# Turns of q and k in score banks, bias parts through DRAM, logits and router steps over groups, w2 casts moved forward

## The chip, the cores and the metric

One core of one Trainium2 chip. The metric is the device time of one execution in microseconds (us). The engines are PE (TensorE, matmuls and transposes), DVE (VectorE), ACT (ScalarE), POOL (GpSimd) and SP (SyncE, which issues the DMAs here).

## What is computed

Four blocks in a row on x of 4 batches x 256 tokens x 512, each added to x. `_layernorm` has no weights.

```python
x = x + attention(_layernorm(x))     # 32 heads of 16, causal, alibi; out @ w_proj + b_proj
x = x + ffn(_layernorm(x))           # 3 experts, top 2
x = x + mlp(_layernorm(x))           # gate/up/down over 1376, smallest half of |silu| set to 0
x = x + ffn(_layernorm(x))           # the same experts and weights again

# attention
scores = einsum('bqhd,bkhd->bhqk', q, k) / 16 + slopes * (k_pos - q_pos)   # causal
out = softmax(scores) @ v
# ffn
modality_ratio = mean(abs(h[:, 76:])) / (mean(abs(h[:, :76])) + 1e-08)     # of each batch
gate_logits = concat([h, modality_ratio]) @ gate_w + gate_b
top_val, top_idx = top_k(softmax(gate_logits), 2)     # weights of each token, normalised
pre = einsum('bsd,edf->ebsf', h, w1) + b1
act = [tanh(pre[0]), gelu(pre[1]), silu(pre[2])]
expert_out = einsum('ebsf,efd->ebsd', act, w2) + b2
# the two experts are those that the batch's first token chooses
```

## The kernel before, in words

All engines run orders written out by hand, and `need(engine, signal, step, k)` makes an engine wait until a signal has been given often enough. What is queued behind a waiting instruction on its engine waits too. 128 tokens are a row (T=8 rows, TB=2 to a batch), 4 heads a group (NG=8 groups to a batch). PSUM has eight banks. Banks 0 to 2 and 3 to 5 are the two score slots (`slot`), banks 6 and 7 are `work`.

**Products in parts.** A projection multiplies float32 in two parts, high (a cast) and low (the difference): `project` (L1566) makes 12 matmuls, `rowsT_hi` by `wqkv_hi`, `rowsT_hi` by `wqkv_lo`, `rowsT_lo` by `wqkv_hi`. ACT makes high parts (`turned_rows` L719, `attention_high` L731, `weight_high` L787), DVE low parts (`turned_rows_low` L979, `attention_low` L991, `weight_low` L1294).

**q and k.** The scores take q and k in three bf16 parts. For each batch PE turns them in four steps (`turn` L1602: f=0 q and f=1 k of the first 16 heads, f=2 and 3 of the last 16). Even steps use `work[0]`, odd ones `work[1]`. ACT casts a turned bank to the first part (L745), DVE subtracts it (`residues` L1007), ACT casts the residue to the second part (`second_part` L752), POOL subtracts that for the third (`cut` L635). `turn(b, 2)` and `turn(b, 3)` wait for the residue that frees their bank, and so does what next uses the bank: `value(0, j)` in batch 0, `project_heads(b-1, j)` afterwards. SP writes the parts to DRAM (`write_cuts` L513) and gathers them back head by head into `qst` and `kst` (`gather` L522), 12 DMAs for each half of the heads.

**A batch.** PE makes the causal scores of each group (`scores` L1635), DVE two row maxima of each (`maxima` L1018). Between groups the value projection, the turn of the heads of the batch before and its low parts, the row turns and q and k of the next batch have their places (`steady` L1155). The maxima are cut, turned in bank 0 and sent by SP into `qst`. Then PE makes transposed scores (`scores_t` L1662), ACT exponentials (L763), PE products with v (`weigh` L1684, two banks in turn) and turns them back (`back` L1699), DVE copies and normalises (`attend` L1040). Ahead of this stand the rest of the next batch's turns and both output projections of the batch before (`project_heads` L1623), whose sums DVE adds to x (`x_plus` L1073). Into the groups of `attend` DVE also takes layer norms, for batch 1 on, and:

- `gate_means` (L1105, batch 0, group 1): two operations over 1536 columns that take the mean off the gate weights.
- `logit_rows` (L1084, groups 4 and 6 of batches 1 to 3): three sums for each row of tokens. A batch's rows are taken in the attention of the next batch. Row 6 and row 7 are taken in the first two expert rows (`ffn_dve` L1361).
- the router of batches 0 and 1 (L1213, L1238, L1260), in groups 2, 3 and 5 of batch 3.

**Biases.** b_proj and b1 enter the products as a matmul with three bf16 parts on partitions 0, 32 and 64 of `bias_proj` and `bias1`. DVE clears `b_raw` (L1133), SP loads both biases into three partitions of it, and `cut_bias` (L1092) makes the parts with six operations, once for 512 and once for 1536 columns, between `query(1, 0)` and the maxima of batch 0.

**Experts.** `ffn_front` (L1731) makes both chosen experts' pre-activations of a row (two blocks of 12 matmuls and a bias), ACT the functions, DVE the mix, PE turns it and `ffn_back` (L1761) multiplies by w2. The first row's front stands ahead of the output projections of batch 3, the w2 casts (L790) and subtractions (L1297) in the first round of `ffn_act` and `ffn_dve`.

## Time and profile before

| | |
|---|---|
| median of 3 runs | 751.97 us (751.32 to 753.47) |
| profiled execution | 751.89 us, its span 750.1 us |
| mean granted PE clock | 0.972 |
| PE busy | 677.2 us (90%) |
| DVE busy | 497.1 us (66%) |
| ACT busy | 333.1 us (44%) |
| POOL busy | 82.6 us (11%) |
| DMA | 51.84 MB, mean 69 GB/s |

The span runs from the first to the last instruction of the profiled execution; its own time is 1.8 us longer. Busy shares are means over stages with different limits, so the stages are read one by one: the attention batches up to about 275 us, the first experts to about 400, the MLP, and the second experts. "Idle before" in a row is how long the engine had nothing to do, with what ended it. The granted clock is a share of full speed.

### The profile page before, as it was taken

What the parts mean: (1) busy time and instruction counts of PE and PEld (TensorE: products, weight loads), DVE (VectorE), ACT (ScalarE), POOL (GpSimd) and SP (SyncE); (2) the same over time, 40 slices, a digit from 0 to 9 for tenths busy, and PEclk for the clock granted to TensorE, in tenths of its full rate; (3) what the DMA queues carried; (4) which work ended last, traced back from release to release, by engine and by line L of the source; (5) the groups of instructions that cost most, each with busy time, mean ns of one, the idle gap of its engine ahead of it and who ended that gap; (6) DMA issues with size and microseconds to landing.
All of it is one profiled execution on the core that took longest, in us unless ns stands there. A gap on an engine that the chain in (4) does not pass through costs nothing.

```text
span 750.1 us, 9861 instructions
## 1 busy us (share of the span) xinstructions
PE 677.2 (90%) x3656; PEld 485.3 (65%) x3656; DVE 497.1 (66%) x916; ACT 333.1 (44%) x510; POOL 82.6 (11%) x185
## 2 busy tenths in 40 slices
PE   5768799889889878899999989999999989999996
PEld 3546467657657656687777746656657546687875
DVE  4678577388468866878678364564562795878655
ACT  4200530441353446252355995674671923525221
POOL 4200200210210101101015000100100210000000
PEclk9899999999999999899999999999999999999999
DMA  8273530350552504000044000000000404000000
GB/s 282 79 215 116 157 99 1 88 170 1 145 188 92 213 1 151 1 0 1 1 151 151 0 1 0 1 0 1 1 1 6 163 0 168 1 15 29 15 29 28
DMA packets 31058, 51.84 MB, mean 69 GB/s; under 512 B 2729, under 2 KB 16425, under 8 KB 29455
## 3 DMA queue, kind: packets, MB, share of 16 engines
q1 hardware_dynamic: 31010, 51.21, 20.7%
q8 instruction: 30, 0.49, 0.3%
q14 instruction: 18, 0.15, 0.1%
HBM read 42.61 MB, written 8.39 MB: 68 GB/s over the span
## 4 chain that ended last, share of the span: by engine, by line
PE 71%; DVE 20%; issue 3%; ACT 3%; DMA 2%; POOL 1%; SPq 0%; ACTq 0%; DVEq 0%; POOLq 0%
PE ps L1781 12%; PE ps L1920 11%; PE ps L1748 11%; PE ps L1981 8%; PE ps L1575 6%; PE ps L1924 5%; DVE nmax L1025 3%; PE ps L1627 2%; DVE junk L1087 2%; PE ps L1689 2%; DMA wqkv_raw<-in_L_attn_a_w_attn 2%; PE ps L1757 2%; DVE nmax L1022 1%; DVE prodT L1510 1%; PE ps L1650 1%
## 5 line engine op out<-in xcount | busy, mean ns | idle before, releaser
L1981 PE MATMUL ps<-wdT,prodT 128*128 128x512 f32 (+1 forms) x176 | 80.1, 612 | 0.3
L763 ACT ACTIVATE probsT<-ps 128x1536 f32<-128x1536 f32 x32 | 45.9, 1450 | 37.8 <-PE ps L1679 37.6
L1981 PEld LDWEIGHTS ps<-wdT,prodT 128*128 128x128 f32 (+1 forms) x176 | 33.8, 196 | 41.9 <-issue 39.7
L802 ACT ACTIVATE funs<-ps 128x512 f32<-128x512 f32 x16 | 9.6, 598 | 97.4 <-PE ps L1750 83.4
L1087 DVE SCALAR_TENSOR_TENSOR junk<-x_sb,gate_row 128x512 f32<-128x512 f32 x48 | 41.5, 865 | 1.6 <-DVE failed L1429 0.3
L1510 DVE COPY prodT<-ps 128x512 f32<-128x512 f32 (+1 forms) x24 | 13.8, 599 | 43.0 <-PE ps L1970 42.7
L647 POOL TENSOR_SCALAR ln_spread<-ln_moments 128x1 f32<-128x1 f32 x24 | 6.0, 250 | 317.5 <-DVE ln_moments L1082 317.4
L1355 DVE SCALAR_TENSOR_TENSOR x_sb<-b_row,coef,x_sb 128x512 f32<-128x512 f32 x48 | 37.9, 790 | 1.7
L1025 DVE TENSOR_REDUCE nmax<-ps 128x4 f32<-128x1024 f32 x32 | 38.8, 1212 | 0.0
L745 ACT CAST parts<-ps 128x512 bf16<-128x512 f32 x16 | 9.4, 587 | 65.1 <-PE ps L1612 64.9
L912 ACT ACTIVATE sign_junk<-mlp_size_next,minus_guess 128x1376 bf16<-128x1376 f32 x24 | 34.6, 1443 | 0.8
L912 ACT ACTIVATE sign_junk<-mlp_size_main,minus_guess 128x1376 bf16<-128x1376 f32 x24 | 34.6, 1442 | 0.8
L1575 PE MATMUL ps<-wqkv_hi,rowsT_hi 128*128 128x512 f32 x96 | 30.4, 442 | 3.5 <-DVE oT_lo L988 1.6
L845 ACT CAST aT_hi<-ps 128x512 fp32r<-128x512 f32 x32 | 17.2, 591 | 34.2 <-PE ps L1757 34.2
L640 POOL TENSOR_TENSOR parts<-resid,parts 128x512 bf16<-128x512 f32 x16 | 18.2, 1162 | 125.4 <-ACT parts L755 125.4
L1689 PE MATMUL ps<-probsT,v_ones 128*32 128x256 f32 x256 | 21.1, 401 | 11.7 <-DVE o_tok L1048 8.4
L1054 DVE COPY outT<-ps 128x256 f32<-128x256 f32 x32 | 13.6, 424 | 26.1 <-PE ps L1694 25.8
L1291 DVE TENSOR_TENSOR aT_lo<-ps,aT_hi 128x512 fp32r<-128x512 f32 x32 | 20.6, 684 | 12.7 <-ACT aT_hi L845 12.6
L1575 PE MATMUL ps<-wqkv_lo,rowsT_hi 128*128 128x512 f32 x96 | 27.3, 407 | 1.1 <-DVE wqkv_lo L993 1.1
L1575 PE MATMUL ps<-wqkv_hi,rowsT_lo 128*128 128x512 f32 x96 | 26.3, 395 | 0.0
L1352 DVE TENSOR_TENSOR x_sb<-ps,x_sb 128x512 f32<-128x512 f32 x16 | 11.1, 691 | 22.6 <-PE ps L1781 22.5
L1679 PE MATMUL ps<-qst,kst 107*128 107x256 bf16 x128 | 25.1, 277 | 0.0
(282 smaller groups left out, 1709.3 us busy)
## 6 DMA issues: line engine op xcount, KB each, us to landing
cuts<-parts SPq DMA_DIRECT2D x16, 384.0 KB, 3.1
qst<-cuts SPq DMA_DIRECT2D x48, 128.0 KB, 2.6
kst<-cuts SPq DMA_DIRECT2D x48, 128.0 KB, 2.6
w_first_raw<-in_L_ffn_w SPq DMA_DIRECT2D x6, 1024.0 KB, 7.8
w_second_raw<-in_L_ffn_w SPq DMA_DIRECT2D x6, 1024.0 KB, 8.5
wqkv_raw<-in_L_attn_a_w_attn SPq DMA_DIRECT2D x3, 1024.0 KB, 9.6
wdT<-in_L_attn_b_w_down SPq DMA_DIRECT2D x1, 2560.0 KB, 10.3
wg_raw<-in_L_attn_b_w_gate SPq DMA_DIRECT2D x1, 2048.0 KB, 8.0
```

The source lines that it names most:

```text
L763: nc.scalar.activation(probsT[:, g % 2, :].rearrange("p (k n) -> p k n", k=3), slot[g % 2], ACT.Exp).then_inc(exp_ok.sem, 1)
L912: nc.scalar.activation(sign_junk[:, :], size_rows(n)[1][:, :], ACT.Sign, bias=minus_guess[:, i:i + 1], accum_out=probe_sum[:, i:i + 1]).th ...
L1025: nc.vector.tensor_reduce(nmax[:, 1, g * G:(g + 1) * G], sl[:, 1:3, :].rearrange("p s (h k) -> p (s h) k", h=2), AX.X, ALU.max, negate=Tru ...
L1087: nc.vector.scalar_tensor_tensor(out=junk[:, :], in0=x_sb[:, t, :], scalar=1.0, in1=gate_v[:, 0:D, e], op0=ALU.mult, op1=ALU.mult, accum_o ...
L1355: nc.vector.scalar_tensor_tensor(out=x, in0=b2_row[:, e, :], scalar=coef[:, n, e:e + 1], in1=x, op0=ALU.mult, op1=ALU.add).then_inc(ffn.b2 ...
L1575: last = nc.tensor.matmul(bank, rows[:, c, at_j], weight[:, n, c, :], start=(i == 0 and c == 0), stop=(i == 2 and c == KC - 1))
L1689: nc.tensor.matmul(o_ps[32 * i:32 * i + 2 * HD, 0:S], v_ones[:, 0, h, :], probsT[:, g % 2, D + i * S:D + (i + 1) * S], start=True, stop=Fa ...
L1748: nc.tensor.matmul(ps[:, 2 * i + s, :], a[:, i, c, :], part[:, e, c, :], start=(k == 0 and c == 0), stop=False)
L1781: last = nc.tensor.matmul(ps[:, Y_BANK, :], a[:, s, c, :], part[:, e[s], c, :], start=(k == 0 and c == 0), stop=(k == len(products) - 1 an ...
L1920: last = nc.tensor.matmul(ps[:, first_bank + q, :], a[:, c, :], part[:, c, at_q], start=(k == 0 and c == 0), stop=(k == 2 and c == KC - 1))
L1924: last = nc.tensor.matmul(ps[:, first_bank + q, 0:IT], row_whole[:, c, :], end[:, c, :], start=(c == 0), stop=(c == KC - 1))
L1981: last = nc.tensor.matmul(ps[:, Y_BANK, :], prodT[0:m, c, :], wdT[0:m, c, :], start=(c == 0), stop=(c == IC - 1))
```

## The change

- The turns of a batch go to four banks of the score slots (2 to 5 in batch 0, 0, 1, 3 and 4 later), the turned maxima to bank 2. A turn waits for no residue; the first two transposed scores of the attention before wait for them. `turn(1, 0)` moves behind `key(1, 1)`. On DVE of batch 0, `query(0, 1)` and `key(0, 1)` come earlier and the residues directly after them.
- In batches 1 and 2 PE makes the first output projection after the second turn, and the second one inside the attention, after the first transposed scores. DVE's x sums stand between the residues.
- The key gathers of batch 0, 12 of 24, are issued by ACT, six ahead of the row casts of batch 1 and six behind them.
- The biases are loaded as 16 columns on 128 partitions, cut there by four DVE operations ahead of `attention_low(1)`, written to DRAM and loaded back as rows.
- `gate_means` is done by ACT in batch 1, in seven operations.
- The logit sums stand one to a group (two more after the last group of batch 1, four behind the last head turns); the last part of the router's weights is a step of its own, one group later.
- At the experts, the first row's front is cut in two around the output projections of batch 3, and ACT's w2 casts and DVE's subtractions come earlier.

```diff
-        maxima_bank = ps[:, 0, :].bitcast(BF16)
+        maxima_bank = ps[:, 2, :].bitcast(BF16)
+        def turn_bank(b, f):
+            return ps[:, (2, 3, 4, 5)[f] if b == 0 else (0, 1, 3, 4)[f], :]
+        def send_rows(eng, b, half, side):
+            stack = (qst, kst)[side]
+            hs = slice(half * H // 2, (half + 1) * H // 2)
+            for t, term in enumerate(TERMS):
+                eng.dma_start(stack[t:TROWS:len(TERMS), hs, :],
+                              cuts[side, half, term[side]].rearrange("(d h) t -> d h t", d=HD)
+                              ).then_inc(scat[half].sem, 16)
...
@@ SP
             load_part(1)
+            sp.dma_start(bias_cols[0:D // NBIAS, :], b_proj.rearrange("(p n) -> p n", n=NBIAS)).then_inc(bias_in, 16)
+            sp.dma_start(bias_cols[D // NBIAS:P, :], b1_in.rearrange("e (p n) -> (e p) n", n=NBIAS)
+                         ).then_inc(bias_in, 16)
             sp.dma_start(x_sb[:, TB:2 * TB, :], x_v[:, TB:2 * TB, :]).then_inc(x_next, 16)
...
-            sp.wait_ge(bias_zero, 1)
+            sp.wait_ge(bias_cut, 4)
+            sp.dma_start(bias_cuts.rearrange("i (p n) -> p i n", p=P), bias_parts[:, :, :]).then_inc(bias_out, 16)
+            sp.wait_ge(bias_out, 16)
+            sp.wait_ge(bias_zero, 2)
             for i in range(3):
-                row = b_raw[32 * i:32 * i + 1]
...
+                sp.dma_start(bias_proj[32 * i:32 * i + 1, :], bias_cuts[i:i + 1, 0:D]).then_inc(bias_rows, 16)
+                sp.dma_start(bias1[32 * i:32 * i + 1, :, :].rearrange("a e n -> a (e n)"),
+                             bias_cuts[i:i + 1, D:]).then_inc(bias_rows, 16)
...
-            gather(0, 0)
-            gather(0, 1)
+            gather(0, 0, (0,))
+            gather(0, 1, (0,))
@@ ACT
-            cut(0, range(4))
+            first_part(0, 0)
+            first_part(0, 1)
+            second_part(0, 0)
+            first_part(0, 2)
+            second_part(0, 1)
+            first_part(0, 3)
+            second_part(0, 2)
+            second_part(0, 3)
+            need(act, cuts_out[0], 0, 16 * 2)
+            send_rows(act, 0, 0, 1)
             turned_rows(1)
+            need(act, cuts_out[1], 0, 16 * 2)
+            send_rows(act, 0, 1, 1)
...
-                cut(b + 1, (0,))
+                if b == 1:
+                    gate_means()
+                first_part(b + 1, 0)
                 maxima(b)
-                cut(b + 1, (1, 2, 3))
+                first_part(b + 1, 1)
+                for f in range(2):
+                    second_part(b + 1, f)
+                for f in range(2, 4):
+                    first_part(b + 1, f)
+                for f in range(2, 4):
+                    second_part(b + 1, f)
                 attend(b)
...
+            need(act, y_ps, B - 1, TB)
+            second_weights(w2_first, 0, (0, 1))
+            ffn_act(ffn1, norm2, route1, lambda: second_weights(w2_first, 0, (2,)), to_mlp)
@@ DVE, attend: what stands in a group
-                    elif b >= 1 and g in (4, 6):
-                        logit_rows(route1, (b - 1) * TB + (g - 4) // 2)
-                    if b == 0 and g == 1:
-                        gate_means()
+                    if b == B - 1:
+                        if g == 2:
+                            router.scores()
+                        elif g == 3:
+                            router.ranks()
+                        elif g in (4, 7):
+                            logit_row(route1, (b - 1) * TB, (g - 4) // 3)
+                        elif g == 5:
+                            router.weights()
+                        elif g == 6:
+                            router.middle_weights()
+                    elif b == 1:
+                        if g in (2, 4, 6, 7):
...
+                    elif b >= 2 and g >= 2:
+                        logit_row(route1, (b - 1) * TB + (g - 2) // E, (g - 2) % E)
...
                 normalise(NG - 1)
+                if b == 1:
+                    for e in (1, 2):
+                        logit_row(route1, (b - 1) * TB + 1, e)
@@ DVE
             for j in range(TB):
                 turned_rows_low(0, j)
+            cut_biases()
             attention_low(1)
...
             key(0, 0)
+            query(0, 1)
             dve.wait_ge(x_next, 16)
             ln_moments_of(1)
-            query(0, 1)
+            key(0, 1)
+            for f in range(4):
+                residue(0, f)
             ln_rows(1)
-            nc.vector.memset(b_raw[0:65, :], 0.0).then_inc(bias_zero, 1)
-            key(0, 1)
-            residues(0)
...
-            cut_bias(0, D, bias_proj[0:65, :], 0)
-            cut_bias(D, NBIAS, bias1[0:65, :, :].rearrange("p e n -> p (e n)"), 6)
...
+                residue(b + 1, 0)
+                residue(b + 1, 1)
                 if b >= 1:
-                    for j in range(TB):
-                        x_plus(b - 1, j)
+                    x_plus(b - 1, 0)
+                residue(b + 1, 2)
+                residue(b + 1, 3)
+                if b >= 1:
+                    x_plus(b - 1, 1)
                 attend(b)
...
                 turned_heads_low(B - 1, j)
+            for e in range(2, 2 + E + 1):
+                logit_row(route1, (B - 2) * TB + e // E, e % E)
...
                 norm_stats(norm2, (B - 1) * TB + j)
+                weight_low(w2_first, w2_high, w2_low, 0, j)
             mix(ffn1, route1, 0, 0)
-            ffn_dve(ffn1, route1, norm3, lambda: second_weights(w2_first, 0), gate_low)
+            ffn_dve(ffn1, route1, norm3, lambda: weight_low(w2_first, w2_high, w2_low, 0, 2), gate_low)
@@ PE
             def value(b, j):
-                if b == 0:
-                    need(pe, res1, b, 3 + j)
...
-                else:
-                    need(pe, res1, b, f - 1)
+                if f % 2 == 0:
+                    need(pe, max_ok, b - 1, 2 * NG - (2, 0)[f // 2])
...
                     need(pe, nmT_ok, b, 1)
+                    if b < B - 1:
+                        need(pe, res1, b + 1, 2)
                 elif g == 1:
                     need(pe, max_ok, b, 2 * NG)
+                    if b < B - 1:
+                        need(pe, res1, b + 1, 4)
...
                     if g < NG:
                         scores_t(b, g)
+                    if g == 0 and 1 <= b < B - 1:
+                        project_heads(b - 1, 1)
...
-                for f in (1, 2, 3):
-                    turn(b + 1, f)
+                turn(b + 1, 1)
...
-                for j in range(TB):
-                    need(pe, res1, b + 1, 3 + j)
-                    project_heads(b - 1, j)
+                project_heads(b - 1, 0)
+                turn(b + 1, 2)
+                turn(b + 1, 3)
                 attend(b)
...
-            ffn_front(ffn1, route1, w1_first, 0, 0)
+            ffn_front(ffn1, route1, w1_first, 0, 0, (0,))
             for j in range(TB):
                 project_heads(B - 1, j)
+            ffn_front(ffn1, route1, w1_first, 0, 0, (1,))
```

The new functions of ACT and DVE:

```python
def gate_means():                       # ACT
    act.wait_ge(gate_in, 32)
    for e in range(E):
        nc.scalar.activation(abs_junk[:, :], gate_v[:, 0:D, e], ACT.Copy,
                             accum_out=gate_sum[:, e:e + 1]).then_inc(gate_ok, 1)
        act.wait_ge(gate_ok, e + 1)
    nc.scalar.mul(gate_mean[:, :], gate_sum[:, :], -1.0 / D).then_inc(gate_ok, 1)
    act.wait_ge(gate_ok, E + 1)
    for e in range(E):
        nc.scalar.activation(gate_v[:, 0:D, e], gate_v[:, 0:D, e], ACT.Identity,
                             bias=gate_mean[:, e:e + 1]).then_inc(gate_ok, 1)

def logit_row(route, t, e):             # DVE
    need(dve, route.logit, t, e)
    if t == 0 and e == 0:
        dve.wait_ge(gate_ok, 2 * E + 1)
    nc.vector.scalar_tensor_tensor(out=junk[:, :], in0=x_sb[:, t, :], scalar=1.0,
                                   in1=gate_v[:, 0:D, e], op0=ALU.mult, op1=ALU.mult,
                                   accum_out=logits[:, t, e:e + 1]).then_inc(route.logit.sem, 1)
```

`cut_biases` is on [128, 16] columns: cast, subtract, cast, subtract into `bias_parts`. `first_part(b, f)` is ACT's cast of L745 on `turn_bank(b, f)`, `residue(b, f)` one step of `residues`, `middle_weights` the last lines of `weights` (from L1283).

## Rows read from the trace of the kernel before

**Rows 1.** Windows of the trace: busy us (x instructions) by engine, PEclk, DMA share, GB/s.

```profile
135.00:138.50 3.50, 3.50 (x9) 2.78 (x10) 0.69 (x1) 1.17 (x2) 2.50 (x3) 0.52 0.97 275
...
340.00:380.00 40.00, 40.00 (x193) 31.74 (x192) 29.21 (x60) 11.63 (x22) 3.59 (x9) 1.00 0.00 0
```

**Rows 2.** Timeline of the opening: start us, us, engine, line, operation, count, idle before.

```profile
28.18 1.43 PE L1612 MATMUL ps<-ident,qk_tok 128*128 128x128 f32 x8 [2.85 <-DVE qk_tok L976]
...
32.74 2.29 POOL L640 TENSOR_TENSOR parts<-resid,parts 128x512 bf16<-128x512 f32 x2 [0.41 <-ACT parts L755]
...
40.13 0.59 ACT L722 CAST rowsT_hi<-ps 128x512 fp32r<-128x512 f32 x1 [6.36 <-PE ps L1562]
...
46.67 0.38 PE L1641 MATMUL ps<-maskS,ident 128*128 128x512 bf16 x1 [2.12 <-DMA kst<-cuts]
...
52.86 1.75 DVE L1102 TENSOR_TENSOR bias<-b_raw,b_p 1x1536 bf16<-1x1536 f32 x1
...
70.81 1.21 DVE L1025 TENSOR_REDUCE nmax<-ps 128x4 f32<-128x1024 f32 x1
```

**Rows 3.** Timeline of SP, the queue that issues the DMAs.

```profile
4.09 2.68 SPq L506 DMA_DIRECT2D kst<-k_alibi  x1
...
36.98 0.59 SPq L529 DMA_DIRECT2D qst<-cuts  x1
...
73.79 1.80 SPq L536 DMA_DIRECT2D qst<-nmaxT  x3
```

**Rows 4.** DMA issues on the page: count, KB each, median us to landing.

```profile
qst<-cuts SPq DMA_DIRECT2D x48, 128.0 KB, 2.6
```

**Rows 5.** Timeline of DVE and PE in the attention of batch 0.

```profile
84.50 2.30 DVE L1108 TENSOR_REDUCE gate_sum<-gate_row 128x3 f32<-128x1536 f32 x1
...
85.04 0.64 PE L1689 MATMUL ps<-probsT,v_ones 128*32 128x256 f32 x8
...
99.77 0.64 PE L1689 MATMUL ps<-probsT,v_ones 128*32 128x256 f32 x8 [0.63 <-DVE o_tok L1048]
```

**Rows 6.** Timeline of PE before the attention of batches 1 and 2.

```profile
130.06 0.60 PE L1612 MATMUL ps<-ident,qk_tok 128*128 128x128 f32 x4
...
135.00 2.04 PE L1627 MATMUL ps<-wproj_hi,oT_hi 128*128 128x512 f32 x4 [1.22 <-issue]
...
147.51 0.64 PE L1689 MATMUL ps<-probsT,v_ones 128*32 128x256 f32 x8
...
197.08 1.19 PE L1627 MATMUL ps<-wproj_hi,oT_hi 128*128 128x512 f32 x4 [1.17 <-DVE resid L1014]
...
200.01 1.29 PE L1627 MATMUL ps<-wproj_hi,oT_hi 128*128 128x512 f32 x4
...
208.10 0.64 PE L1689 MATMUL ps<-probsT,v_ones 128*32 128x256 f32 x8
```

**Rows 7.** Timeline of PE in the attention of batch 1.

```profile
156.52 0.64 PE L1689 MATMUL ps<-probsT,v_ones 128*32 128x256 f32 x8
...
159.65 0.64 PE L1689 MATMUL ps<-probsT,v_ones 128*32 128x256 f32 x8 [0.80 <-DVE o_tok L1048]
...
164.55 0.44 PE L1702 MATMUL ps<-ident,outT 128*128 128x128 f32 x2 [0.73 <-DVE outT L1054]
```

**Rows 8.** Timeline of PE in the attention of batch 3.

```profile
264.92 0.64 PE L1689 MATMUL ps<-probsT,v_ones 128*32 128x256 f32 x8
...
275.54 0.66 PE L1620 MATMUL ps<-ident,o_tok 128*128 128x128 f32 x4 [0.62 <-DVE o_tok L1048]
```

**Rows 9.** Timeline of the first expert rows, ACT, DVE and PE.

```profile
292.27 5.53 ACT L790 CAST w_first_hi<-w_first_raw 128x2048 fp32r<-128x2048 f32 x3
...
294.79 6.69 DVE L1297 TENSOR_TENSOR w_first_lo<-w_first_raw,w_first_hi 128x2048 fp32r<-128x2048 f32 x3
...
306.04 3.47 PE L1781 MATMUL ps<-w_first_hi,aT_lo 128*128 x8 [2.05 <-DVE aT_lo L1291]
...
311.20 1.09 PE L1748 MATMUL ps<-w_first_hi,hT_hi 128*128 x4
```

More of the change, by code:

```diff
@@ L520, in write_cuts, with gather @@
                                  ).then_inc(cuts_out[half].sem, 16)
[L522 removed]
+            def gather(b, half, sides=range(2)):
                 need(sp, sT_ps, b - 1, (half + 1) * GHALF)
                 need(sp, cuts_out[half], b, 16 * 2)
[L526 to L531 removed]
+                for side in sides:
+                    send_rows(sp, b, half, side)
             def send_maxima(b):
@@ L1850, in _ @@
             key(1, 1)
+            turn(1, 0)
             maxima(0)
```

145 lines of the change are left out of this document (58 added, 87 removed).

## The prediction, made before the changed kernel ran

> **What bounds the kernel now.** I read the page first, then the windows, then the timeline of each stage between its waits. From about 311 us on the matrix engine (PE) hardly pauses: in [rows 1] it is busy for all 40.00 us of one stretch at a granted clock of 1.00. The change leaves that part alone, so a gain has to come from the stages ahead of it, where PE waits. The other row of [rows 1] shows what a pause costs afterwards: PE works through all 3.50 us, but at clock 0.52, after short pauses. I price that as half speed for 3.5 us, so about 1.7 us lost.
>
> In the opening [rows 2] PE's second turn stands until 28.18 (2.85 idle) for a VectorE (DVE) add that sits behind other work. GpSimd ends its last third part at 35.03. ScalarE (ACT) casts the rows of batch 1 at 40.13. The first scores wait for the gathers until 46.67. DVE then is busy with the bias cuts until 54.61, although scores lie ready from about 47.9, and the last maximum of batch 0 ends at 72.02.
>
> **The change, part by part.** The sum is made against the profiled execution's 751.89 us (span 750.1 and 1.8 around it). The median of the runs, 751.97, is 0.1 away, so nothing is corrected for it.
>
> *1. Opening, to the last maximum of batch 0.* The four turns go to banks of their own. The second needs only the key sum, which now has neither the normalisation nor a memset ahead of it, so it starts near 25.6 instead of 28.18, 2.6 earlier. The chain behind it (cast, residue, cast, GpSimd) is paced by GpSimd's 1.15 per part, as before, so the last part ends 35.03-2.6=32.4. SP writes it out, and gathers can start at about 33.2, against 36.98 [rows 3]. ACT now issues six of half 0's twelve gathers, then casts the rows of batch 1, then issues six more. At SP's spacing, 0.59 and a gap, 0.63 each, the six take 3.8, and ACT reaches the casts at 37.0 (40.13 before). PE has finished values and row turns near 34.4; it stands until the low parts are there, 1.3 after the casts began, at 38.3. After 3.9 us of rest I charge the 1.7 above. One 12-matmul block takes 2.93 (197.08 to 200.01 in [rows 6]), so the query block ends at 38.3+2.9+1.7=42.9, when the gathers have landed (37.0 and 2.6 [rows 4]). The scores start 3.7 earlier than 46.67, and 1.3 later, at 44.3, DVE starts the maxima, since the bias cuts are now four operations on 16 columns ahead of the second weight cut, where DVE stands for a cast anyway; if that cover fails they cost under 1 us. PE then has the key block (2.9), scores, and the query block (2.9) between the groups, so DVE's fourth group starts at 53.6. Five groups at 1.75 end at 62.3. Against 72.02 that is **-9.7**. The two new small loads ahead of the third weight load cost at least nothing and at most the 0.5 of an issue; I take +0.2, as the queue is backed up (the 2.68 issue [rows 3]). The bias rows' way through DRAM uses SP before 28, with nothing behind it.
>
> *2. Attention of batch 0.* Today two gate operations stand on DVE, the first at 84.50 for 2.30 [rows 5]; PE's third group of products is at 85.04 and the last, five groups on, at 99.77. Undisturbed, a group takes (156.52-147.51)/4=2.25 [rows 6, 7], so five take 11.25: 85.04+11.25=96.3. **-3.5**. ACT does the seven replacements in batch 1, while it waits for the turns at 130.06 and has no other work. The largest six are on 512 columns, as the 0.59 cast of [rows 2]; at up to 1 us each they take some 6, and without that cover the turns' casts would come later by that.
>
> *3. Before the attention of batches 1 and 2.* Today the four turns of the next batch share two banks, each waiting for a residue; both output projections come after them, and the exponentials after both. Afterwards, counted from the first turn at 130.06 [rows 6]: second turn at 131.0 (DVE's key sum, as now), ends 131.6; first projection to 134.6; two turns to 135.7; scores to 136.8; second projection to 139.75; meanwhile ACT finishes its cuts at 137.8 and has the first exponential at 139.3; next scores to 140.85; first products, third scores, and the second products at 142.7. Today they are at 147.51: **-4.8**. Batch 2 has no slow clock today (135.00 to 147.51 is 12.5, 197.08 to 208.10 is 11.0): **-3.3**. The late item next is the last cut, 1.6 later than now; its gather has a whole attention before it is needed.
>
> *4. Logits spread.* Six logit sums now stand in two blocks of three and hold PE, as at 159.65 (0.80) and 164.55 (0.73) [rows 7]; without them seven groups and a turn end 1.1 earlier than 164.55. Batch 1 still has two sums after its last group, 1.9 of DVE ahead of the next maxima, of which 0.8 reaches PE: -0.3. Batch 2: -1.1. **-1.4** together.
>
> *5. Batch 3 to the third expert row.* The sixth group is at 264.92 [rows 8]; two more at 2.25 put the eighth at 269.4, and the head turns, 3.35 behind it (DVE has one logit sum there), at 272.75 instead of 275.54, 2.8 less. PE then does half the first expert row, both output projections, the other half: the same twelve-matmul blocks in another order. ACT starts the w2 casts at once after the projections, 1.84 each [rows 9], and DVE its subtractions, 2.23 each, but the first of these stands between the two x sums and waits for the cast. So the second row's low part comes only near 293.6, no earlier than today, and PE stands 3.7 and loses clock. What is gained lies behind: the third subtraction ends 297.7 and not 301.48, the a-low parts come at 302.4 where PE waits until 306.04, and the third row's front starts at 306.2 against 311.20. **-5.0**, the 2.8 included.
>
> Sum: -9.7+0.2-3.5-4.8-3.3-1.4-5.0=-27.5, and 751.89-27.5=724.4.
>
> **A price I can't see.** No DMA is issued by ACT today. From below: 0.25 less per issue than SP's would save under 2 us. From above stands the 2.68 issue with a full queue [rows 3]. I take SP's 0.63: three issues of the maxima, each of a few rows, also take 1.80 together, so the time doesn't look like one per row moved. The Trainium skill, "DMA: Bandwidth & Descriptors", HWDGE ordering, speaks against it: SP and ACT have rings of their own, but no DMA engine or descriptor generator of their own. By that rule the two streams would alternate, and the time would be the 728.4 of the first rival; no row here can test it.
>
> **Rivals.**
> - *The two issue streams alternate.* The twelve gathers of half 0 take 7.6 instead of 3.8, ACT casts at 40.8, and query, scores and all behind them are 3.8 to 4.0 later: 728.4. For it: nothing here shows two streams at once, and at 128 KB each 0.63 the engines are already well used. Against: the 1.80 above. Chance 0.22.
> - *The front of the experts gives its share back.* DVE, standing for a w2 cast with the second x sum, the first mix and the low part behind it, becomes the bound, and the -5.0 is 0: 729.4. Chance 0.12.
> - *The turns do not do what they should.* If the first two scores of an attention wait for the residues as long as the turns do now, part 3 brings nothing: 732.5. Against it: ACT is free there. Chance 0.04.
> - *ACT's issues cost 2.68.* Casts at 33.2+16.1=49.3, the last key gather at 34.4+32.2+2.6=69.2 where the fifth scores want it at 53.5: 15.7 lost, 740.1. Chance 0.04.
> - *Slower.* The same place with issues so slow that ACT is the bound: the point is 34.4+12x+2.6=53.5+27.5, x=3.7 us each. At 4 us: 755.4. For it there is only the 2.68 row, which is below the point. Chance 0.03.
>
> **The numbers.** The forecast has 0.55. Its own error, one slow-clock stretch more or less in each of three places and the small waits that I rounded, is about 5 to either side; to the high side the range takes in the first three rivals, so 717 to 736. A measurement of this kernel can tell about 0.3% (2.3 us) from no change; all cases but the last are faster by more: 0.95, and between lies 0.02.
>
> **What would show it.** Right: the last maximum of batch 0 at 61 to 64; products of batch 0 evenly 2.25 apart; the second products 12.6 after the first turn in batches 1 and 2; the third expert row's front 5 us nearer to batch 3's first products. Wrong: ACT's gathers over 0.7 apart, the casts of batch 1 after 39, PE standing on DVE in batch 1's first groups, or front and low parts of the second row later than now by more than 1 us.

## The result and the profile after

The changed kernel took 721.37 us, median of 4 runs (720.54 to 722.49); the kernel before, on the same chip beside it, 752.72 us (751.32 to 756.62). The ratio is 0.957, 95% interval 0.954 to 0.961. The profiled execution took 721.25 us, of which 719.5 are the span; the mean granted clock was 0.984 (0.972 before). PE is busy for 664.0 us (677.2 before) and DVE for 484.1 (497.1).

To see where the time went, both timelines are cut at eight instructions that each kernel has: the end of the last maximum of batch 0, the start of the last group of products in batches 0, 1 and 2, the end of the last maximum of batch 3, the first head turn of batch 3, the start of the third expert row's front, the end. All in us:

| stretch | before | after | difference | predicted |
|---|---|---|---|---|
| to the last maximum of batch 0 | 72.02 | 62.80 | -9.22 | -9.5 |
| attention of batch 0 | 27.75 | 23.79 | -3.96 | -3.5 |
| to the last products of batch 1 | 61.73 | 56.06 | -5.67 | -5.1 |
| to the last products of batch 2 | 60.60 | 55.76 | -4.84 | -4.4 |
| scores of batch 3 | 23.17 | 22.47 | -0.70 | 0 |
| attention of batch 3, to the head turns | 30.27 | 27.12 | -3.15 | -2.8 |
| to the third expert row's front | 35.66 | 33.78 | -1.88 | -2.2 |
| the rest | 438.90 | 437.72 | -1.18 | 0 |
| span | 750.1 | 719.5 | -30.6 | -27.5 |

The opening, in the timeline of the changed kernel (start us, us, engine, line, operation, count, idle before); it answers to [rows 2] and [rows 3]:

```profile
25.67 1.53 PE L1662 MATMUL ps<-ident,qk_tok 128*128 128x128 f32 x12 [0.35 <-DVE qk_tok L1013]
...
32.98 4.13 ACTq L491 DMA_DIRECT2D kst<-cuts  x6
...
33.15 8.09 SPq L491 DMA_DIRECT2D qst<-cuts  x12
...
37.16 0.58 ACT L734 CAST rowsT_hi<-ps 128x512 fp32r<-128x512 f32 x1 [5.87 <-issue]
...
38.52 2.07 PE L1627 MATMUL ps<-wqkv_hi,rowsT_hi 128*128 128x512 f32 x4 [3.62 <-DVE rowsT_lo L1019]
...
43.81 0.45 PE L1691 MATMUL ps<-maskS,ident 128*128 128x512 bf16 x1
...
45.25 0.69 DVE L1057 TENSOR_REDUCE nmax<-ps 128x4 f32<-128x512 f32 x1 [0.51 <-PE ps L1700]
...
61.59 1.21 DVE L1060 TENSOR_REDUCE nmax<-ps 128x4 f32<-128x1024 f32 x1
```

The turns run in one piece. ACT's six gathers take 4.13 us, 0.69 each, while SP sends twelve in 8.09, 0.67 each: the two issue streams run side by side. Then the casts, 3.62 us of rest for PE, the query block, and the first maximum 9.4 us earlier than the end of the bias cuts in [rows 2] (54.61). The window of that rest and block has the low clock, and full DMA engines (busy us of PE, PE's weight loads, DVE, ACT and POOL, then PEclk, DMA share, GB/s):

```profile
36.00:44.00 8.00, 5.47 (x13) 3.97 (x14) 1.29 (x2) 1.07 (x2) 0.00 (x0) 0.57 1.06 237
```

PE in the attention of batch 0 and ahead of that of batch 1, for [rows 5] and [rows 6]:

```profile
86.59 0.64 PE L1743 MATMUL ps<-probsT,v_ones 128*32 128x256 f32 x8 [0.63 <-DVE o_tok L1083]
...
118.25 1.18 PE L1677 MATMUL ps<-wproj_hi,oT_hi 128*128 128x512 f32 x4
...
123.25 1.18 PE L1677 MATMUL ps<-wproj_hi,oT_hi 128*128 128x512 f32 x4
...
129.53 0.64 PE L1743 MATMUL ps<-probsT,v_ones 128*32 128x256 f32 x8
```

Neither projection waits, and the second products are 12.64 behind the first turn (116.89), 17.45 before. The way to the third expert row, for [rows 8] and [rows 9]:

```profile
248.00 1.09 PE L1670 MATMUL ps<-ident,o_tok 128*128 128x128 f32 x8 [1.19 <-DVE o_tok L1083]
...
261.07 2.29 DVE L1344 TENSOR_TENSOR w_first_lo<-w_first_raw,w_first_hi 128x2048 fp32r<-128x2048 f32 x1 [3.32 <-ACT w_first_hi L810]
...
268.92 1.86 PE L1802 MATMUL ps<-w_first_hi,hT_lo 128*128 x4 [3.43 <-DVE hT_lo L1338]
...
281.78 1.09 PE L1802 MATMUL ps<-w_first_hi,hT_hi 128*128 x4
```

DVE stands 3.32 us for a w2 cast, with the second sum of x, the mix and the low part of the second row behind it, and PE then stands 3.43 for that low part.

### The profile page after: what moved, and what is told of

It reads as the page before. It is cut to its first block, busy times and chain, and to the rows that moved or that the text cites. A ratio compares the mean times of both kernels' runs of the same rounds, so it can differ in the third digit from the quotient of the medians.

```text
span 719.5 us, 9856 instructions
## 1 busy us (share of the span) xinstructions
PE 664.0 (92%) x3656; PEld 480.4 (67%) x3656; DVE 484.1 (67%) x905; ACT 338.8 (47%) x520; POOL 81.1 (11%) x185
## 3 DMA queue, kind: packets, MB, share of 16 engines
q10 hardware_dynamic: 384, 1.57, 1.0%
## 4 chain that ended last, share of the span: by engine, by line
PE 77%; DVE 14%; DMA 2%; ACT 2%; issue 2%; SPq 1%; POOL 1%; ACTq 1%; DVEq 0%; POOLq 0%
PE ps L1835 13%; PE ps L1974 12%; PE ps L1802 12%; PE ps L2035 10%; PE ps L1627 7%; PE ps L1978 5%; DVE nmax L1060 3%; PE ps L1677 2%; PE ps L1743 2%; PE ps L1811 2%; DVE nmax L1057 1%; PE ps L1733 1%; DVE prodT L1561 1%; PE ps L1700 1%; PE ps L1804 1%
## 5 line engine op out<-in xcount | busy, mean ns | idle before, releaser
L2035 PE MATMUL ps<-wdT,prodT 128*128 128x512 f32 (+1 forms) x176 | 78.5, 602 | 0.4
L659 POOL TENSOR_SCALAR ln_spread<-ln_moments 128x1 f32<-128x1 f32 x24 | 7.7, 321 | 301.5 <-DVE ln_moments L1131 301.4
L884 ACT CAST aT_hi<-ps 128x512 fp32r<-128x512 f32 x32 | 17.2, 590 | 37.3 <-PE ps L1811 37.3
L1057 DVE TENSOR_REDUCE nmax<-ps 128x4 f32<-128x512 f32 x32 | 21.9, 683 | 4.7 <-PE ps L1700 4.7
```

Source lines behind the costliest of these rows:

```text
L2035: last = nc.tensor.matmul(ps[:, Y_BANK, :], prodT[0:m, c, :], wdT[0:m, c, :], start=(c == 0), stop=(c == IC - 1))
```

## The experiments

Twelve kernels ran, each one the changed kernel with the edit shown. The table has the median of the runs and the stretches of the profiled run, cut as above (b0 to b3 are the batches, max. and att. the last maximum and the attention). The kernel before took 751.5 to 752.7 us beside them.

| run | median | max. b0 | att. b0 | b1 | b2 | scores b3 | att. b3 | experts' front | rest |
|---|---|---|---|---|---|---|---|---|---|
| changed kernel | 721.37 | 62.80 | 23.79 | 56.06 | 55.76 | 22.47 | 27.12 | 33.78 | 437.7 |
| e1 gathers all on SP | 721.14 | 63.62 | 23.79 | 56.02 | 55.75 | 21.99 | 27.10 | 33.62 | 437.1 |
| e2 casts early | 724.77 | 64.52 | 23.78 | 56.01 | 55.78 | 23.67 | 27.11 | 35.26 | 437.1 |
| e3 bias cut on DVE | 731.84 | 72.19 | 24.52 | 56.00 | 55.75 | 21.95 | 27.09 | 33.75 | 438.9 |
| e4 gate means on DVE | 727.04 | 62.85 | 27.49 | 55.97 | 55.75 | 26.55 | 27.11 | 35.00 | 439.2 |
| e5 logits in blocks | 728.01 | 63.13 | 24.48 | 56.79 | 57.10 | 23.03 | 29.74 | 35.29 | 437.1 |
| e6 both projections first | 732.43 | 64.56 | 23.79 | 57.63 | 57.37 | 27.27 | 27.11 | 34.96 | 439.2 |
| e7 turns on shared banks | 731.10 | 62.39 | 23.89 | 60.78 | 59.06 | 21.96 | 27.11 | 34.78 | 439.0 |
| e8 w2 late | 723.51 | 62.50 | 23.79 | 56.04 | 55.73 | 22.92 | 27.11 | 35.46 | 439.0 |
| e9 e6, loads after gathers | 724.61 | 64.50 | 23.79 | 57.61 | 57.33 | 22.05 | 27.12 | 33.71 | 438.9 |
| e10 opening | 723.33 | 62.30 | 24.45 | 56.03 | 55.74 | 26.66 | 27.12 | 34.94 | 439.2 |
| e11 experts' front | 717.38 | 62.46 | 23.79 | 56.02 | 55.73 | 22.11 | 27.12 | 28.51 | 439.9 |
| e12 together | 714.64 | 60.76 | 24.53 | 56.01 | 55.75 | 21.97 | 27.11 | 28.49 | 437.0 |

The middle stretches repeat within 0.1 us where an edit leaves them alone (batch 1: 55.97 to 56.06 in nine kernels). Others do not. The opening of e6 and e9 is late as a whole: the second turn starts at 27.3 and 27.2 and not at 25.3 to 25.8, with PEclk 0.83 in e6's window 14 to 24 us (1.00 in the changed kernel). Both have the same order of PE in later batches and no other kernel here has it; whether that makes their opening late is open. Counted from that turn, openings without an edit take 36.7 to 37.5 us to the last maximum. The attention of batch 0 has 23.8 or 24.5, the scores of batch 3 lie between 21.9 and 23.7 or near 27, the front of the experts between 33.6 and 35.3, and the rest between 437.0 and 439.9. So an edit is judged by its own stretch, against the spread of that stretch; the medians carry some luck of the others. The profiled run is one of the four to six, and not always a middle one: 731.61 in e4 and 728.14 in e10, each the slowest of its kernel.

### The opening: gathers, casts, bias parts

**e1, all gathers of batch 0 on SP.**

```diff
-            gather(0, 0, (0,))
-            gather(0, 1, (0,))
+            gather(0, 0)
+            gather(0, 1)
...
-            send_rows(act, 0, 0, 1)
             turned_rows(1)
-            send_rows(act, 0, 1, 1)
```

> All 24 gathers of batch 0 on SP again, everything else as changed. Theory A (what the changed kernel's profile suggests): the scores of batch 0 start at 43.81 because the query block ran at the low clock after PE's 3.62 us of rest, and this rest was caused by the casts of batch 1 standing behind ACT's six gathers. With all on SP the casts are at about 34.5, the query block ends before 40, and the scores wait for the last of half 0's twelve gathers: 33.15 + 12 x 0.63 + 2.6 = 43.3. So sharing the gathers is worth next to nothing as it was done: 720.8 to 721.6, scores at 43.3 to 43.8. Theory B (the prediction's working: halving the issue time is what moved the start of the scores): about 3.8 us of gathers more, scores near 47.5, 725.

Measured: 721.14 us (ratio to before 0.959, 0.954 to 0.965), scores at 43.10, behind a wait of 4.25 us for the gathers. Theory A. The issue rows of the window 32 to 48 us, the changed kernel's first (count, KB each, median us from issue to landing):

```profile
kst<-cuts ACTq DMA_DIRECT2D x12, 128.0 KB, 6.3
qst<-cuts SPq DMA_DIRECT2D x12, 128.0 KB, 6.8
```

and those of e1:

```profile
qst<-cuts SPq DMA_DIRECT2D x12, 128.0 KB, 2.7
kst<-cuts SPq DMA_DIRECT2D x12, 128.0 KB, 2.6
```

Two queues issue twice as fast, and each gather then takes about 2.5 times as long to land. From the turns to the last maximum e1 takes 37.94 us, 0.8 more than the changed kernel (37.13) and 0.4 to 1.2 more than the openings without an edit: sharing the gathers brings about that, and the medians are the same. The last gather of the first half lands at 42.96 in e1 and at 43.51 in the changed kernel, the last of all at 50.46 and 50.38.

**e2, the casts between ACT's second and third gather.**

```diff
-            send_rows(act, 0, 0, 1)
+            send_rows(act, 0, 0, 1, range(2))
             turned_rows(1)
+            send_rows(act, 0, 0, 1, range(2, 6))
```

> ACT sends two of its six gathers of half 0, casts the two rows of batch 1, then sends the other four; everything else as changed. Theory A: casts at about 34.5 and not 37.16, PE rests under 2 us before the query block and keeps its clock, the block ends at about 39.5, the gathers of half 0 are all issued at 38.2 and land by 40.8; scores at about 41 and not 43.81, the last maximum of batch 0 2 to 2.8 us earlier: 718.5 to 719.4. Theory B (the DMA engines, with both streams on them, are the bound of the landing, not the issue): scores stay at 43 to 44 and the time at 721.

Measured: 724.77 us. The scores start as theory B says, and my theory A was wrong; the time is 3.8 above theory B's. The query block is done at 39.1, and PE waits for the gathers instead:

```profile
43.48 0.58 PE L1693 MATMUL ps<-maskS,ident 128*128 128x512 bf16 x1 [4.38 <-DMA kst<-cuts]
```

The window 40 to 48 has clock 0.57 and a DMA share of 1.04. The scores start 0.33 earlier than in the changed kernel, but the low clock now falls on the key block behind them, where DVE waits for it, and not on a query block that nobody needed before 43.5: 38.76 us from the turns to the last maximum, 1.6 more. The other 2.7 stand where nothing was edited: 1.2 in the scores of batch 3, where PE waits 1.53 for a gather, and 1.5 in the front of the experts. Here the rest that was taken away from a place where it was covered came back where it was not.

**e10, half 0 alone first, and the key block ahead of the scores.**

```diff
+            need(sp, scat[0], 0, scat[0].per)      # SP, and the same on ACT
             gather(0, 1, (0,))
...
             query(1, 0)                            # PE, and the same on DVE
+            key(1, 0)
             scores(0, 0)
-            key(1, 0)
```

(with e2's order of the casts)

> Batch 0's first half is gathered by both queues (ACT sends two, casts the rows, sends four), its second half is issued only when the first has landed, and PE does the key block of batch 1 ahead of the first scores, where it stands now, DVE its sum ahead of the maxima. Theory A (with two streams the DMA engines are full, at 240 GB/s and a landing of 6.3 to 6.8 us against 2.6 with one, so the second half's gathers delay the first): half 0, 1.57 MB, lands by 41.5 and not 43.3, PE has no rest over 2 us before the scores and keeps its clock, the maxima start by 43.2 and run 1.74 apart but for one gap: last maximum at 58.5 to 59.5 and not 62.80: 717 to 718.2. Theory B (the landing of the first half does not depend on the second): scores at 43.3, last maximum at 60 to 60.8, 718.5 to 719.5. Theory C (the second half comes too late for the fifth scores): last maximum after 61, 720 or more.

Measured: 723.33 us, 36.72 from the turns to the last maximum: 0.4 less than the changed kernel, but within the 36.7 to 37.5 of the openings without an edit, so no gain is shown. PE's waits for gathers:

```profile
43.03 0.38 PE L1694 MATMUL ps<-maskS,ident 128*128 128x512 bf16 x1 [1.33 <-DMA kst<-cuts]
...
53.21 0.39 PE L1694 MATMUL ps<-maskS,ident 128*128 128x512 bf16 x1 [1.78 <-DMA kst<-cuts]
```

Half 0 lands at 42.90 although no gather of half 1 is on its way: theory B for the first half, and theory C for the second, which comes 1.78 late. The last gather of half 0 lands at 42.96, 43.34 and 42.90 in e1, e2 and e10, with the issues of its twelve gathers ending at 40.9, 37.5 and 37.3. With two queues the engines are the bound: the DMA share is 1.0 there at about 240 GB/s, and by that rate I estimate 6.5 us for the 1.57 MB of half 0 alone, behind what is left of the cuts, the last of which lands at 36.11. With one queue it is the issue: in the window 36 to 44 us e1 has 213 GB/s at a share of 0.67, the changed kernel 237 at 1.06. The Trainium skill says it in "DMA: Bandwidth & Descriptors", HWDGE ordering: SP and ACT have rings of their own on the same DMA engines. The traces agree for the landing (6.3 to 6.8 against 2.6 us); for the issue they show no alternation (0.69 and 0.67 us side by side), which was my reading and not the page's words.

**e3, the bias parts cut on DVE** from one row for each part, between the query sum of batch 1 and the first maximum, as before.

```diff
             query(1, 0)
+            cut_bias(0, D, bias_proj[0:65, :], 0)
+            cut_bias(D, (1 + E) * D, bias1[0:65, :, :].rearrange("p e n -> p (e n)"), 6)
...
-            cut_biases()
```

> The bias parts cut on DVE from one row each as in the kernel before, between the query sum of batch 1 and the first maximum; everything else as changed. Theory A (the cut stood on the path by itself): it takes DVE 7.9 us from about 44.7, the maxima start at about 52.6 and not 45.25, and some of it is caught up, as groups are now 1.74 apart and PE has two groups ready: last maximum of batch 0 at 68 to 70 and not 62.80, so +5 to +7: 726.5 to 728.5. Theory B (PE's key and query blocks between the groups pace the maxima anyway): under +2.5, 721.4 to 723.9.

Measured: 731.84 us (ratio 0.972, 0.967 to 0.976), the last maximum at 72.19. DVE and PE in e3:

```profile
44.59 0.41 DVE L1149 CAST b_p<-b_raw 65x512 bf16<-65x512 f32 x1
...
52.25 1.75 DVE L1157 TENSOR_TENSOR bias<-b_raw,b_p 1x1536 bf16<-1x1536 f32 x1
54.03 0.69 DVE L1059 TENSOR_REDUCE nmax<-ps 128x4 f32<-128x512 f32 x1
...
55.91 0.61 PE L1709 MATMUL ps<-maskS,ident 128*128 128x512 bf16 x1 [6.93 <-DVE nmax L1062]
```

The cuts take 9.4 us and nothing of it is caught up: PE rests 6.93, then its query block runs at the low clock and DVE stands for that. Theory A, at more than its price. 72.19 is the 72.02 of the kernel before: with the bias cuts on DVE, the early turns and the shared gathers bring the opening nothing. None of the 9.2 us is there without the move of the bias parts; what that move would bring alone was not run.

### The attentions

**e4, the gate's means on DVE in batch 0** (two operations in the second group, ACT's seven removed).

> The gate's means taken off on DVE in the second group of batch 0's attention, as in the kernel before (two operations), and not on ACT in batch 1; everything else as changed. Theory A: PE's products of batch 0 are again 3.4 to 3.9 us longer from third to last (13.1 to 14.7 and not 10.86), all of it on the path: 724.8 to 725.3. Theory B: ACT's seven operations cost batch 1 something now, so that taking them away there gives part of it back: first products of batch 1 less than 3 us later, under 724.

```profile
75.23 2.29 DVE L1148 TENSOR_REDUCE gate_sum<-gate_row 128x3 f32<-128x1536 f32 x1
77.56 1.76 DVE L1151 SCALAR_TENSOR_TENSOR gate_row<-gate_sum,gate_row 128x1536 f32<-128x1536 f32 x1
```

The attention of batch 0 is 3.70 us longer (27.49), batch 1 is 0.09 shorter: theory A, and ACT's operations are free in batch 1. They take 101.86 to 107.89, 6.0 us, and ACT then has 9.69 idle. The median, 727.04, is 2 us above that price. The profiled run, the slowest, has 4.1 us more in the scores of batch 3 (see e6); whether the other runs have part of that is open.

**e5, the logit sums in two blocks.**

```diff
-                    elif b >= 2 and g >= 2:
-                        logit_row(route1, (b - 1) * TB + (g - 2) // E, (g - 2) % E)
+                    if b >= 1 and g in (4, 6):
+                        logit_rows(route1, (b - 1) * TB + (g - 4) // 2)
```

> The logit sums again in two blocks of three, at the fifth and seventh group of an attention; everything else as changed. Theory A: each block makes two groups late, 1.6 to 1.8 us for an attention of batches 2 and 3; batch 1 loses the same but wins back the 0.5 us of its two trailing sums: +3.5 to +4.5 together, 725 to 726. Theory B (the prediction's own figure: 0.3, 1.1 and the 1.8 of batch 3's two groups counted elsewhere): spread without the tail's part is worth 1.4, 722.8. Theory C: no change, DVE has slack: 721.4.

Measured: 728.01 us. Batch 1 is 0.73 longer, batch 2 1.34, batch 3's attention 2.62: 4.7 together, theory A by its mechanism and a little over its range. The median is 2 us over it. Another 1.5 is in the front of the experts, where the block after the head turns ran at the low clock (4.50 us to the projections and not 2.94).

**e6, both projections ahead of the third turn.**

```diff
                 project_heads(b - 1, 0)
+                project_heads(b - 1, 1)
                 turn(b + 1, 2)
```

(and none inside the attention)

> Both output projections ahead of the third turn in batches 1 and 2, none between the first two groups of scores; the turns keep their own banks; everything else as changed. Theory A: the second projection then stands ahead of the first scores and so of the first exponential, but the exponential was covered by it: the second products come 0.8 to 1.2 later in each of the two batches: 723.0 to 723.8. Theory B (the whole 3.0 us of a projection lands on the path): +6, 727. Theory C (ACT's last cuts are the bound, not PE): no change.

Measured: 732.43 us, more than any theory. The edit's own stretches show 1.57 and 1.61 (57.63 and 57.37). The scores of batch 3 are 4.8 longer. SP and PE there, and the window behind:

```profile
188.93 1.73 SPq L553 DMA_DIRECT2D w_first_raw<-in_L_ffn_w  x2
192.58 4.49 SPq L491 DMA_DIRECT2D qst<-cuts  x6
...
206.77 0.61 PE L1691 MATMUL ps<-maskS,ident 128*128 128x512 bf16 x1 [2.20 <-DMA kst<-cuts]
```

```profile
206.00:210.00 4.00, 3.23 (x15) 2.55 (x16) 0.41 (x2) 0.00 (x0) 0.18 (x1) 0.53 0.73 219
```

Two expert weight loads of 1 MB stand in the queue ahead of batch 3's gathers. PE waits 2.20 us for the last key gather (0.33 in the changed kernel) and then works at the low clock (0.53). The wait alone does not decide on the clock; e2 and e4 at the same place:

```profile
202.85 0.39 PE L1693 MATMUL ps<-maskS,ident 128*128 128x512 bf16 x1 [1.53 <-DMA kst<-cuts]
```

```profile
204.80 0.61 PE L1702 MATMUL ps<-maskS,ident 128*128 128x512 bf16 x1 [1.51 <-DMA kst<-cuts]
```

After the same wait e2 keeps a clock of 1.00 (202 to 206 us) and takes 23.67 for the stretch, 1.2 more than the changed kernel; e4 has 0.53 (204 to 208 us) and takes 26.55.

**e9, e6 with those loads behind the gathers of the first half.**

```diff
-                if b + 1 == B - 1:
-                    need(sp, k_ps, B - 1, TB)
-                    load_experts(w1_in, w1_first[0], w1_here, (0, 1))
                 gather(b + 1, 0)
+                if b + 1 == B - 1:
+                    need(sp, k_ps, B - 1, TB)
+                    load_experts(w1_in, w1_first[0], w1_here, (0, 1))
```

> Both projections ahead of the third turn, as in the run before that cost 11 us, and in addition the two 1 MB loads of expert weights issued after the gathers of batch 3's first half and not ahead of them. Theory A: of the 11 us only about 2 were the projections (second products 1.2 and 1.0 later); 5.3 were batch 3's first scores, which stood 2.20 us for the last key gather, queued behind those loads, and then ran with the next block at the low clock; the rest is clock in the expert layers. With the loads behind the gathers PE does not wait for a gather there: last maximum of batch 3 within 22.5 of the last products of batch 2 (27.3 in that run, 22.5 in the changed kernel), time 723 to 726.5. Theory B (the late write of the cut parts, not the loads, makes the gathers late): still over 25 and 729 or more.

Measured: 724.61 us, the scores of batch 3 in 22.05: theory A. In e9's trace the gathers go first, at the same time as in e6, and the first scores stand for nothing (the fifth 0.36 us for a gather):

```profile
192.47 3.67 SPq L491 DMA_DIRECT2D qst<-cuts  x6
196.18 3.75 SPq L491 DMA_DIRECT2D kst<-cuts  x6
199.97 2.08 SPq L553 DMA_DIRECT2D w_first_raw<-in_L_ffn_w  x2
```

```profile
204.29 0.38 PE L1691 MATMUL ps<-maskS,ident 128*128 128x512 bf16 x1
```

So e6 is 3.2 us of projections, an opening 1.6 late and a trap that the edit only sprang: the same 4 to 5 us stand in e4 (26.55) and e10 (26.66), whose edits touch nothing there. SP issues there as in the changed kernel, but the last gather lands 1.2 to 1.3 later, counted from the last products of batch 2. One of e6's four runs took 725.73 and the others 732.3 to 733.6, and e10's spread from 720.0 to 728.1, as if the gathers were in time in some executions; that no run without a profile can show.

The trap comes with the change itself. SP's row of the two loads in the kernel before and in the changed one:

```profile
200.49 1.75 SPq L541 DMA_DIRECT2D w_first_raw<-in_L_ffn_w  x2
```

```profile
182.58 1.71 SPq L553 DMA_DIRECT2D w_first_raw<-in_L_ffn_w  x2
```

The last products of batch 2 start at 222.10 and 198.41. So the loads went out 21.6 us ahead of that start and now go out 15.8 ahead, and the last gather of batch 3's first half landed 0.9 us ahead of it and now lands 1.5 behind. With the turns on shared banks again (e7) it is 20.7 and 0.5 ahead, and PE waits for no gather of q or k there.

**e7, the turns of batches 1 to 3 on two shared banks**, each waiting for a residue, then both projections, as before.

```diff
-            return ps[:, (2, 3, 4, 5)[f] if b == 0 else (0, 1, 3, 4)[f], :]
+            return ps[:, (2, 3, 4, 5)[f] if b == 0 else (6, 7, 6, 7)[f], :]
```

> From batch 1 on, the turns on two shared banks, each waiting for a residue, then both projections, as in the kernel before; batch 0 and everything else as changed. Theory A (part 3 of the prediction): second products 3.3 to 4.8 us later after the first turn in batches 1 and 2, 16.0 to 17.4 and not 12.6: 728.0 to 729.5. Theory B (only the place of the projections counts, so the same as with both projections ahead): 723 to 724.

Measured: 731.10 us, batch 1 longer by 4.72 and batch 2 by 3.30, the prediction's 4.8 and 3.3: theory A. In batch 1 the waits for residues are back, and the first projection is at the low clock:

```profile
118.59 0.66 PE L1656 MATMUL ps<-ident,qk_tok 128*128 128x128 f32 x4 [0.46 <-DVE resid L1046]
119.59 0.66 PE L1656 MATMUL ps<-ident,qk_tok 128*128 128x128 f32 x4 [0.34 <-DVE resid L1046]
121.47 2.05 PE L1671 MATMUL ps<-wproj_hi,oT_hi 128*128 128x512 f32 x4 [1.22 <-issue]
```

With e6, the 8.0 us divide: 3.2 for the second projection between the groups of scores, 4.8 for the banks and the order that they allow. Of the 4.8, 1.4 is the difference between the two batches, and only batch 1 has the low clock.

### The front of the experts

**e8, casts and subtractions of w2 at their old place**, the first row still cut in two.

> The casts and subtractions of the first experts' second weights at their old place; the first expert row stays cut in two around the projections; everything else as changed. Theory A: the third row's front comes 1.9 to 2.2 us later after batch 3's head turns (33.9 and not 32.0 after the first front): 723.3 to 723.6. Theory B: the order is worth nothing, as DVE ends the same operations at the same time: 721.4. Theory C: early subtractions are a loss, as they hold the low part of the second row (PE stands 3.43 for it), and the late place is faster: 719 to 721.

Measured: 723.51 us, the stretch 35.46: 1.68 longer than in the changed kernel and 0.2 shorter than the 35.66 of the kernel before. Theory A, slightly under, but kernels without an edit here lie between 33.62 and 35.29. So the size of the gain from the early w2 work is not shown better than 0.2 to 1.8, and that of the cut front can't be told from nothing. What e8 shows is where PE stands: not for the low part of the second row, but 3.04 for the a-high parts and 1.27 for the a-low parts:

```profile
277.86 3.78 PE L1836 MATMUL ps<-w_first_hi,aT_lo 128*128 x8 [1.27 <-DVE aT_lo L1340]
```

**e11, another order on DVE.**

```diff
             for j in range(TB):
                 x_plus(B - 1, j)
                 need(dve, x_add, B - 1, j + 1)
                 norm_stats(norm2, (B - 1) * TB + j)
-                weight_low(w2_first, w2_high, w2_low, 0, j)
-            mix(ffn1, route1, 0, 0)
+                logit_row(route1, T - 2, j)
+            weight_low(w2_first, w2_high, w2_low, 0, 0)
```

(in the loop the low part of the second row comes next, then the mixes, then the other two subtractions; the other four logit sums go to the next row)

> DVE's order behind batch 3's attention: both sums of x with their statistics first (two logit sums in between), then the first w2 subtraction, the low part of the second row at once behind it, the mixes, the other two subtractions; the remaining four logit sums after the low parts of the third row. Theory A (PE's 3.43 us for the low part of the second row, and the low clock after it, are the loss that is left): no rest there, third front 29.6 to 30.5 after the head turns and not 33.78: 717.2 to 718.5. Theory B (DVE's total is the bound of these two rows): the wait only moves to the a-low parts or to the fourth row, under 1 us gained: 720.5 to 721.5.

Measured: 717.38 us (ratio 0.954, 0.950 to 0.959), the stretch 28.51 and not 33.78. In e11's trace:

```profile
264.56 1.09 PE L1809 MATMUL ps<-w_first_hi,hT_lo 128*128 x4
...
275.74 1.09 PE L1809 MATMUL ps<-w_first_hi,hT_hi 128*128 x4
...
284.36 0.66 PE L1788 MATMUL ps<-ident,h_cur 128*128 128x128 f32 x4 [0.70 <-DVE tiny L1253]
```

Theory A, by 5.3 us where I expected 3.3 to 4.2: with the wait also the low clock behind it is gone. DVE did the same work in another order, with both sums of x ahead of the w2 subtractions and the low part behind only the first of them. The median gained 4.0, as the rest is 439.9 in this profile; e12, with the same order there, has 437.0.

**e12, together:** e11 (the sums' copy one mix earlier), the key block first, e2's casts with the second half sent at once, and e9's loads.

> What the runs so far point to, together: DVE's order behind batch 3's attention as in the run that had it alone (with the copy of the router's sums one mix earlier, for which PE stood 0.70 there); the key block of batch 1 ahead of the first scores, the casts between ACT's second and third gather, the second half's gathers again sent at once (the run that held them back waited 1.78 for them at the fifth scores); the two weight loads behind the gathers of batch 3's first half. Theory A (the pieces add): last maximum of batch 0 at 60.0 to 60.6 and not 62.80, third front 28.5 after the head turns, no PE wait on a gather in batch 3, 713.3 to 715.5, under every kernel here. Theory B (what is won ahead is given back at batch 3's gathers or to the clock in the expert layers): no better than the tail's order alone, 716.5 to 719.

Measured: 714.64 us, median of 6 runs (712.77 to 718.52), ratio to before 0.949 (0.946 to 0.953), where the changed kernel has 0.957: the fastest kernel here, theory A. In its trace:

```profile
43.56 0.38 PE L1701 MATMUL ps<-maskS,ident 128*128 128x512 bf16 x1 [0.16 <-DMA qst<-cuts]
...
274.62 1.09 PE L1812 MATMUL ps<-w_first_hi,hT_hi 128*128 x4
```

The last maximum comes at 60.76 (expected 60.0 to 60.6, so a little late; 35.05 from the turns, 2.1 less than in the changed kernel), the front of the experts takes 28.49, and the scores of batch 3 21.97.

## Why the prediction was right, and where it was not

The predicted 724.4 us stands 3.0 above the measured median, inside the range, and seven of the eight stretches came out within 0.7 us of their term.

- **Opening.** -9.5 predicted, -9.22 measured, and turns (25.67), casts (37.16) and the end of PE's rest (38.52) came within 0.2 us. But one step is wrong: "when the gathers have landed (37.0 and 2.6 [rows 4])". The last of them lands at 43.51 and not at 39.6, since a landing of 2.6 us holds for one stream and not for two. It did not show, because the query block, at the low clock, kept PE until 43.81: I had charged 1.7 for that clock, and it took 2.4. That is luck, two errors that covered each other, and e2 took the cover away. The scores start 2.9 earlier than before and not 3.7. That earlier start brings nothing while the bias cuts stand on DVE (e3), and sharing the gathers has 0.4 to 1.2 of it (e1). The 0.2 for the two small bias loads fits: without them (e3) the second turn starts at 25.32 and not at 25.6 to 25.8.
- **The first rival, alternating streams,** falls as it was written: ACT issues at 0.69 us. Its idea holds one stage later, in the engines, and there both ways of sending end at the same time (50.38 and 50.46 in e1).
- **Batch 0.** -3.5 predicted, -3.96 in the profile, 3.70 when undone alone. ACT's seven operations took the 6 us that I gave them and were hidden.
- **Ahead of the attentions.** 4.8 and 3.3 predicted, 4.72 and 3.30 by e7. This is the best confirmed part, and e6 says that the place of the second projection is 3.2 of it. What I did not see is that it also brings the 1 MB loads nearer to batch 3's first scores: they are 5.8 us nearer, 4.9 of it by e7 (see e9).
- **Logits.** The terms of 0.3 and 1.1 were too small: e5 shows 0.73 and 1.34, and 2.62 in batch 3. I took groups at 2.25 us apart; from the second products to the last turn there are 15.28 and 15.78 us in batches 1 and 2, so 1.8 and 1.3 less than before (17.04 and 17.06) and not 1.1, as the last group comes 1.86 behind the seventh.
- **Front of the experts.** 2.2 predicted behind the head turns, 1.88 measured, 1.68 undone, in a stretch that differs by up to 1.7 between kernels that are equal there; the size is confirmed no better than that. The wait for the second row's low part that I forecast at 3.7 is there at 3.43. I took it as given; e11 shows that it was the larger prize, 5.3 us.
- **Not in the sum:** 0.70 in the scores of batch 3 and 1.18 in the rest. No term of the prediction stands for either, and both differ by more than that between kernels that are equal there (21.95 to 27.27, and 437.0 to 439.9). Which part of either is the change's is open.
- **The last rival's time** is added up wrongly: 34.4+48+2.6-53.5 is 31.5, which gives 755.9 and not 755.4. Nothing hangs on it.

## What to carry to other kernels

Before transfers are split over two queues, ask how much more the window can move. Here one queue moved 213 GB/s and two 237: the second queue halved the issue and lengthened the landing, so what waits for the landing gained next to nothing. The DMA share with one queue, 0.67, did not show that. An engine that waits in order for a late input holds everything behind it, so put what others need ahead of the wait (5.3 us for another order of the same operations on DVE). A bulk load that stands ahead of a transfer on the path may cost nothing in one profile and 5 us in the next. A wait of 0.3 us for a gather is a sign that there is no margin left, and a change that makes an earlier stage shorter can bring it about.

## What was not expected of the hardware

- Two issue streams ran side by side at 0.67 and 0.69 us per gather of 128 KB, nearly as fast as one alone (0.64 in e1), while the median landing went from 2.6 and 2.7 to 6.3 and 6.8 us.
- A rest of 1.65 us (e10) or 2.20 us (e6) of PE ahead of batch 3's scores was followed by the low clock: PEclk 0.53 in the window 206 to 210 of e6. In the changed kernel the rest there was 0.33 and the clock stayed at 1.00. Such a wait cost 4 to 5 us altogether, more than twice its length. But 1.51 us were followed by the low clock in e4 and 1.53 by full speed in e2, where the wait cost 1.2.
- The same rest of 1.18 to 1.19 us ahead of the head turns was followed by full speed in the changed kernel (2.94 us for the block behind it) and by the low clock in e2 (4.48 us). In this place the clock can't be foretold from the rest alone, and it moves a time by 1.5 us.
